# Second layer of a two-layer model: key mask built by ScalarE, low half of the token heads taken by VectorE, and another order of the steps

## What is computed

```python
# layer two, cross-attention
scores = jnp.where(causal_mask, neg_inf, scores)
scores = jnp.where(key_padding_mask, neg_inf, scores)
x = x + tanh(g) * (softmax(scores) @ v) @ Wo.T
# layer two, token mixture: w is (tokens, 16), rows sum to 1
q, k, v = [einsum('ne,neh->nh', w, einsum('nc,ech->neh', x, p)) for p in projections]
o = softmax(q k^T / sqrt(h)) @ v
out = einsum('enh,ehc->nc', einsum('ne,nh->enh', w, o), o_proj)
```

## Time and profile before

| | us |
|---|---|
| median of 3 runs | 1639.06 |
| lowest and highest of them | 1631.96, 1639.1 |
| time of the profiled execution | 1626.43 |
| its span from the first to the last instruction | 1624.7 |

### The profile page before, as it was taken

How to read it: one execution, slowest core, us unless ns; L and a number is a source line. 1 busy time by engine, 2 the same in 40 slices (tenths; PEclk the granted TensorE clock), 3 DMA queues, 4 the chain that set the end, 5 groups by cost and what they waited for, 6 DMA issues and landing times.

```text
span 1624.7 us, 52801 instructions
## 1 busy us (share of the span) xinstructions
PE 1513.6 (93%) x17129; PEld 1308.8 (81%) x17130; DVE 1293.3 (80%) x4044; ACT 1064.2 (65%) x2661; POOL 1186.9 (73%) x1715
## 2 busy tenths in 40 slices
PE   5899999976999789999999999999999999999996
PEld 4666666755999469888888888888888888889885
DVE  3777778863555378998999889988998999988885
ACT  3777777743556456767766776677667766776664
POOL 4556666642456568888888888888888888888785
PEclk9999999986999999999999999999999999999998
DMA  2322222234553100000000000000000000000000
GB/s 78 110 72 74 78 78 78 78 102 120 147 140 91 29 16 15 20 16 15 21 19 17 15 21 15 21 15 21 15 21 15 17 19 21 15 15 18 5 8 11
DMA packets 92108, 69.05 MB, mean 42 GB/s; under 512 B 13937, under 2 KB 87697, under 8 KB 91921
## 3 DMA queue, kind: packets, MB, share of 16 engines
q1 hardware_dynamic: 76512, 49.34, 10.3%
q0 software_dynamic: 5120, 12.62, 2.4%
q10 hardware_dynamic: 10288, 4.74, 1.1%
...
## 4 chain that ended last, share of the span: by engine, by line
PE 79%; issue 7%; DVE 6%; ACT 3%; DMA 2%; POOL 2%; SPq 1%; POOLq 0%; ACTq 0%; DVEq 0%
PE s_bank L1998 12%; PE s_bank L1999 11%; PE s_bank L2000 11%; PE tb L1815 6%; PE po L1945 4%; PE s_bank L1933 4%; PE s_bank L1795 4%; PE po L1829 3%; PE m L1769 2%; PE s_bank L2146 2%; PE s_bank L1804 2%; ACT pT L889 1%; DVE qkv L1552 1%; DMA kx<-kT 1%; PE s_bank L2133 1%
## 5 line engine op out<-in xcount | busy, mean ns | idle before, releaser
L745 POOL TENSOR_TENSOR qkv<-qkv,scaled 128x384 f32<-128x384 f32 x480 | 489.4, 1020 | 87.2 <-ACT scaled L1020 37.8
L1020 ACT ACTIVATE scaled<-s_bank,wg 128x384 f32<-128x384 f32 x449 | 260.3, 584 | 114.5 <-PE s_bank L2000 109.9
L1998 PE MATMUL s_bank<-proj_hi,hn_hi 128*128 128x384 f32 x900 | 327.0, 363 | 5.6 <-DVE qkv L1552 5.6
L1552 DVE SCALAR_TENSOR_TENSOR qkv<-s_bank,wg,qkv 128x384 f32<-128x384 f32 x449 | 273.9, 610 | 49.8 <-PE s_bank L2000 39.6
L1999 PE MATMUL s_bank<-proj_lo,hn_hi 128*128 128x384 f32 x900 | 302.9, 337 | 0.0
L2000 PE MATMUL s_bank<-proj_hi,hn_lo 128*128 128x384 f32 x900 | 302.2, 336 | 0.0
L889 ACT ACTIVATE pT<-tb 128x512 f32<-128x512 f32 x256 | 152.9, 597 | 136.1 <-PE tb L1815 134.5
L1998 PEld LDWEIGHTS s_bank<-proj_hi,hn_hi 128*128 128x128 f32 x900 | 169.4, 188 | 18.9 <-DVE qkv L1552 14.1
L1815 PE MATMUL tb<-ident,prob 128*128 128x128 f32 x1024 | 161.4, 281 | 15.2 <-ACT pT L889 13.8
L1999 PEld LDWEIGHTS s_bank<-proj_lo,hn_hi 128*128 128x128 f32 x900 | 170.2, 189 | 1.6
L2000 PEld LDWEIGHTS s_bank<-proj_hi,hn_lo 128*128 128x128 f32 x900 | 169.0, 188 | 0.0
...
...
## 6 DMA issues: line engine op xcount, KB each, us to landing
...
kx<-kT SPq DMA_DIRECT2D x256, 32.0 KB
...
```

Source lines behind the costliest of these rows:

```text
L745: g.tensor_tensor(into, into, scaled[m % SCALED][:, 0:cols], ALU.add).then_inc(dense_added, 1)
L1020: ins = act.activation(into, bank[:, 0:3 * D], ACT.Copy, scale=wg[v % 4][:, 1, k:k + 1])
L1552: v.scalar_tensor_tensor(out=acc, in0=bank[:, 0:3 * D], scalar=wg[w % 4][:, 0, k:k + 1], in1=acc, op0=ALU.mult, op1=ALU.add).then_inc(dens ...
L1998: pe.matmul(bank[:, 0:cols], hi[:, tile], of(proj_hi), start=True, stop=False)
```

## The change

It does three things in layer two. The mask tile is made by ScalarE with four operations for a unit (`mask_unit`), each the causal tile times a column `pad_keep` plus a column `pad_off`; GpSimd's `pad_row`, with its tiles `not_causal` and `pad_unit`, is gone. `ohT` is gone: ScalarE copies the heads once, and VectorE subtracts `oh_hi` from the bank (`lower_heads`). And all four `body1` are written in another order. What is computed stays the same.

```diff
+            def mask_unit(v):
+                if exists(v):
+                    q = s[1]
+                    if exists(v - 2):
+                        act.wait_ge(q["scores_in_psum"], 4 * v - 4)
+                    for n in range(4):
+                        ins = act.activation(mask_keys[v % 2][:, n, :], causal[:, :], ACT.Identity,
+                                             bias=pad_off[:, 4 * v + n:4 * v + n + 1],
+                                             scale=pad_keep[:, 4 * v + n:4 * v + n + 1])
+                    ins.then_inc(q["pad_row_ready"], 1)
...
             zero_rows(act, range(4, E0))
             act.wait_ge(setup["pad_in_psum"], 1)
-            act.activation(pad_keys[:, :], tb[:, 0:SEQS], ACT.Copy).then_inc(setup["pad_keys"], 1)
+            act.activation(pad_off[:, :], tb[:, 0:SEQS], ACT.Copy, scale=MASKED)
+            act.activation(pad_keep[:, :], tb[:, 0:SEQS], ACT.Identity, bias=onesf[:, 0:1], scale=-1.0)\
+                .then_inc(setup["pad_keys"], 1)
+            act.wait_ge(setup["pad_keys"], 1)
+            mask_unit(0)
+            mask_unit(1)
...
             def token_heads(v):
                 if exists(v):
                     act.wait_ge(f["o1_in_psum"], v + 1)
-                    act.activation(oh_hi[:, :], m1[:, 0:256], ACT.Copy)
-                    act.activation(ohT[:, :], m1[:, 0:256], ACT.Copy).then_inc(f["o1_ready"], 1)
+                    act.activation(oh_hi[:, :], m1[:, 0:256], ACT.Copy).then_inc(f["o1_ready"], 1)
...
             exp_bank(1, 3)
             copy_pT(q, 1, 1)
+            mask_unit(3)
             apply_second_norm(1, 0, lambda t: x3[0][:, t, :], lambda t: hn[:, t, :])
...
+            def lower_heads(w):
+                if exists(w):
+                    v.wait_ge(f["o1_ready"], w + 1)
+                    v.tensor_tensor(oh_lo[:, :], m1[:, 0:256], oh_hi[:, :], ALU.subtract).then_inc(f["oh_lo_ready"], 1)
```

The same order change on GpSimd, whole:

```diff
             def body1(u):
+                if exists(u + 3):
+                    residual(1, u + 3, (u + 1) % 2)
+                add(u - 1, "o", 2)
+                hidden_length(u + 1)
+                add(u - 1, "o", 3)
                 add(u, "q", 1)
-                hidden_length(u + 1)
                 gather(u + 4)
-                add(u, "q", 2, 3)
-                if u == 0:
-                    residual(1, 3, 1)
-                if u > 0:
-                    pad_row(u + 3)
-                lower_hidden(u + 1)
-                add(u, "q", 4, 5, 6, 7, 8, 9, 10)
-                lower_heads(u - 1)
-                add(u, "q", 11, 12, 13)
+                add(u, "q", 2, 3, 4, 5)
                 if exists(u + 4):
                     norm(1, u + 4)
-                add(u, "q", 14, 15)
-                add(u, "o", 1)
+                add(u, "q", 6, 7, 8, 9)
+                lower_hidden(u + 1)
+                add(u, "q", 10)
+                add(u, "q", 11, 12, 13)
+                add(u, "q", 14)
                 hidden_norm(u + 2)
-                add(u, "o", 2)
-                if exists(u + 4):
-                    residual(1, u + 4, u % 2)
-                add(u, "o", 3)
+                add(u, "q", 15)
+                add(u, "o", 1)
```

210 lines of the change are left out of this document (92 added, 118 removed).

## The result

The changed kernel is slower. Its median of five runs is 1651.69 us (1636.19 to 1655.43) against 1636.17 us of before (1631.96 to 1639.1, also five runs): a ratio of 1.0089, 95% interval 1.0050 to 1.0128. A second comparison gave 1.0078 (1.0047 to 1.0109).

A forecast was written before the change was run, and what follows sets the result against it. TensorE was taken to bound layer two. Per unit -0.52 + 0.10 + 0.20 = -0.22 us, -5.7 us over 26 units, with +1.9 at the ends -3.8 us; stated 1635 us against a median of 1639.06, range 1624 to 1656.

The forecast's parts named there:

- The first rival: VectorE ends last at the first output part; half of 1.4 us late gives +0.38 us a unit, 1651 us; chance 0.27.
- The removed stall, -0.52 us: The high-half token part's wait for VectorE's take, 0.52 us in each of 26 units, goes.
- The work moved off GpSimd is worth nothing by itself: GpSimd loses 2.3 us a unit but doesn't end the stall; VectorE only has fewer operations locking it out.
- the masks cost ScalarE nothing: Four mask operations, 1.1 to 1.5 us a unit, fit ScalarE's 10 us of idle time, made one unit ahead.
- The masks' wait, +0.10 us: Start of a unit: room before the masks shrinks from 0.41 to 0.06 us; new stall 0 to 0.15, taken as 0.10.
- The first output part, +0.20 us: End of a unit: TensorE waits there for ScalarE's chain, which ends last; 0.20 us with the restart of weight loads.
- ScalarE's chain: Scaling of part 12, `oh_hi`, subtraction, take 14 and handovers: 2.2 us against 2.1 us of token parts on TensorE.
- 1.4 us for waits that shrink: VectorE's port waits ahead of part 14: about 0.8 us less at L1531, some 0.6 at gate steps and group sums.
- The 1.0 us that VectorE would no longer wait for TensorE: Waiting inside VectorE's 22.37 us, first maximum to part 14, taken off: 22.37 + 2.45 - 1.0 = 23.8 us.
- Filling and emptying, +1.9 us: Both ends of layer two: +1.1 us for `mask_unit(3)` ahead of the second norm, +1.3 and -0.5 in the last units.
- The +1.3 and -0.5: Last units: token maximum behind the group sums costs 1.3 us; last low half on VectorE, one copy fewer, saves 0.5.
- The third rival: GpSimd's additions queue behind the second norm, so turning matmuls and group sums wait; each 0.3 us a unit costs 8; chance 0.07.

The follow-up runs named there:

- b_res: Kernel before with VectorE's result of unit u-3 moved behind the last maximum, a pause of VectorE; ratio to before 0.9977.
- b_mask: Kernel before in its own order, with only the masks moved from GpSimd to ScalarE; ratio to before 1.0005.
- b_both: Kernel before in its own order, with masks moved to ScalarE and the low half of the token heads to VectorE; 1642.4 us, ratio to before 1.0050.
- a_thin_late: Changed kernel with GpSimd's adds of parts 9 and 10 and `hn_lo` cut to one column from the fourth unit on; ratio to before 1.0037.
- a_thin_early: Changed kernel with GpSimd's adds of parts 6, 7 and 8 cut to one column from the fourth unit on; ratio to before 1.0049.

## Why the prediction was wrong

The direction was missed: -0.22 us a unit and +1.9 us at the ends were forecast, +0.15 us a unit and +9.3 us at the ends (filling 4.3, the unit behind the middle 1.0, emptying 4.0) were measured. The first rival's time, 1651 us, is what came, by luck: it had 10 us for the middle, where 3.8 were lost, and counted from 1639.06 us, while the median of five runs of before is 1636.17. The unit, 32.86 us, lies inside the 32.3 to 32.9 that the forecast would have let pass.

- *The removed stall, -0.52 us.* Right: it is gone, 0.48 us by the starts of the matmuls. b_res shows that it was worth having.
- *The work moved off GpSimd is worth nothing by itself, the masks cost ScalarE nothing.* Right, by b_mask: 1.0005. The low half was costed at 0.45 us; with 0.38 us that was no error, but the prediction asked only what is queued behind it on VectorE. It also frees bank m1, and in the order of before the move costs 0.15 us a unit (b_both), 1.0050 against 1.0005 in all.
- *The masks' wait, +0.10 us.* Right in kind and size: 0.12.
- *The first output part, +0.20 us.* This is the step of the middle that failed: VectorE ended last and not ScalarE's chain, and 0.48 us was the price. The sum had VectorE's stretch at 23.8 us with the port waits of before and took off 1.4 us for waits that shrink, which left 22.4, the same as TensorE's 22.4. Measured are 22.64 us, and another 0.15 from the end of the take to the product, where the sum had nothing; TensorE without the stall would be there at 22.39 (22.79 less 0.40). The take ends 0.25 us behind that and the handover adds 0.15: the 0.40.

  Two terms were wrong inside that sum. The 1.0 us that VectorE would no longer wait for TensorE went, but its pauses in that stretch fell by only 0.25 us (1.74 to 1.49), since a pause of 0.7 us for the gather came in. And the port waits did not shrink where they were set to: L1531 lost 1.20 us (0.8 assumed) and L1467 0.83, but of the floor and mask steps of the gate and the sums of the groups, which were to lose 0.6 together, the floor gained 0.46, `gate_mask` 0.26 and the group total 0.33, and only `gate_idle` lost, 0.48. The shift of the logits gained 0.76 and the division 0.57 (all as means of 26 units). The selection (0.68) and the last gate step (0.49) gained too, behind part 14. All in all VectorE's time grew by 0.43 us a unit, and 0.38 of it is the subtraction: the waits moved and their sum stayed.

  The forecast's 0.20 us for ScalarE's chain was a good figure for what comes next: with GpSimd cut short that chain is last, at 0.10 us and 0.08 for the restart. That a handover costs 0.05 us, as the chain's sum has it, no run shows.
- *Filling and emptying, +1.9 us.* The step with the largest miss. The two steps named are there (the second norm of unit 0 starts 0.8 us later after the first masks, 1.5 in the second profile; the maximum stands behind the group sums). The +1.3 and -0.5 don't quite follow from their rows, which give +1.6 and -0.7; that changes nothing. Not looked at were the norm of unit 2 in body 1 (1.49 us), where four adds of GpSimd lie ahead, and the body of unit 30 in the emptying, which alone is 2.9 us longer, 2.2 of them by the order. Part of the filling's 4.3 us is a lower granted clock, whose cause stays open. An order that fits four units in flight was not followed through the bodies with fewer. The third rival, GpSimd's queue ahead of the second norm, had its place there and not in the middle.

The Trainium skill ("SBUF — State Buffer", section "SBUF: two separate sides") has it that of a GpSimd operation and a VectorE one that need the shared port pair the first to start keeps it to its end. a_thin_late agrees for the division: 0.42 us with GpSimd's neighbour cut short, 1.01 with it whole. Who starts first can't be read here where it matters: the two starts are recorded 0.02 us apart in the changed kernel (1184.06 and 1184.08, VectorE waits) and 0.01 apart in a_thin_early (1174.32 and 1174.33, VectorE goes through).
